# Decoder layer on one core: the second norm's row statistics are computed later, and six instead of four groups of a transpose go over DMA

## The reference

```python
x = x + attn(layernorm(x), w_qkva, gamma)          # stage 1
x = x + xattn(layernorm(x), context, Wq, Wkv, null_kv, Wout, ln_scale, ln_bias)
x = x + ffn(layernorm(x), w_gate, w_up, w_down)

def layernorm(x, eps=1e-5): return (x - mean(x)) / sqrt(var(x) + eps)
def attn(x, w_qkva, gamma):
    xn = x / max(norm(x), 1e-12) * sqrt(256) * gamma
    q, kv, a = split(xn @ w_qkva, 3)
    a = sigmoid(a)                                  # h[t] = a[t] * h[t-1] + kv[t] along the 1024 rows
    return q * scan(a, kv)
def xattn(x, context, ...):                         # 16 heads of 64, 64 context rows and a null key
    ...                                             # softmax(q k^T / 8) v, Wout, a layer norm of the result
def ffn(x, ...):                                    # ternary weights, rows quantised to 8 bits
    ...                                             # down(silu(gate(x)) * up(x))
```

## Time and profile before

| what | value |
|---|---|
| runs | 485.0, 485.03, 488.04 us; median 485.03 |
| profiled execution, its own time | 486.71 us |
| its span, first to last instruction | 484.8 us, so 1.9 us lie around it |
| mean granted TensorE clock | 0.992 |
| busy: PE, DVE, ACT, POOL | 94%, 84%, 71%, 70% of the span |
| chain that ended last | PE 81%, DVE 6%, POOL 5% |

### The profile page before, as it was taken

How to read it: one execution, slowest core, us unless ns; L and a number is a source line. 1 busy time by engine, 2 the same in 40 slices (tenths; PEclk the granted TensorE clock), 3 DMA queues, 4 the chain that set the end, 5 groups by cost and what they waited for, 6 DMA issues and landing times.

```text
span 484.8 us, 8018 instructions
## 1 busy us (share of the span) xinstructions
PE 455.8 (94%) x2520; PEld 358.9 (74%) x2548; DVE 407.0 (84%) x882; ACT 343.0 (71%) x442; POOL 341.5 (70%) x495
## 2 busy tenths in 40 slices
PE   1999999999999999999999999999999999999674
PEld 0777888877877788787877878778787777876332
DVE  4689998997755888998998989989899898997784
ACT  4456756757735456888888888888888888887460
POOL 2234458978880678888878788787887778878850
PEclk9999999999999999999999999999999999999988
DMA  8995014463000000023214222121221312212254
GB/s 262 325 372 212 1 26 63 87 125 94 1 1 1 1 1 11 7 49 45 49 39 51 49 45 49 40 60 39 43 50 39 61 39 45 50 39 62 49 119 89
DMA packets 75577, 33.82 MB, mean 70 GB/s; under 512 B 58128, under 2 KB 73744, under 8 KB 75536
## 3 DMA queue, kind: packets, MB, share of 16 engines
q1 hardware_dynamic: 75536, 33.31, 28.9%
HBM read 15.21 MB, written 4.19 MB: 40 GB/s over the span
## 4 chain that ended last, share of the span: by engine, by line
PE 81%; DVE 6%; POOL 5%; DMA 2%; ACT 2%; issue 2%; another core or an unknown queue 0%; SPq 0%; POOLq 0%; DVEq 0%; ACTq 0%
PE psum L1429 32%; PE psum L1465 12%; PE psum L1713 10%; PE psum L1718 10%; PE psum L1451 3%; PE psum L1690 3%; PE psum L1698 3%; PE psum L1580 2%; PE psum L1561 2%; PE psum L1500 2%; DMA gcol<-in_L_attn_gamma_dram 1%; PE psum L1543 1%; DMA region_d<-region_d 1%; PE psum L1710 1%; PE psum L1484 1%
## 5 line engine op out<-in xcount | busy, mean ns | idle before, releaser
L672 POOL TENSOR_TENSOR region_d<-region_d,rden 128x1024 f32<-128x1024 f32 x30 | 57.1, 1905 | 13.5 <-DVE rden L1230 13.1
L1713 PE MATMUL psum<-VW,region_d 128*128 128x256 f32 x256 | 60.7, 380 | 0.2
L1718 PE MATMUL psum<-VW,region_d 128*128 128x256 f32 x256 | 60.5, 379 | 0.0
L1210 DVE TENSOR_REDUCE mx<-psum 128x8 f32<-128x512 f32 x64 | 44.0, 687 | 13.1 <-PE psum L1429 12.0
L1429 PE MATMUL psum<-Mhi,xT2hi 128*128 128x512 f32 x128 | 53.5, 418 | 0.9 <-DVE xT2lo L1186 0.9
L1718 PEld LDWEIGHTS psum<-VW,region_d 128*128 128x128 f32 x256 | 48.6, 190 | 6.6
L1255 DVE SCALAR_TENSOR_TENSOR region_c<-psum,hzw,region_c 128x1024 f32<-128x1024 f32 x32 | 41.1, 1283 | 13.6 <-ACT region_c L910 13.3
L1713 PEld LDWEIGHTS psum<-VW,region_d 128*128 128x128 f32 x256 | 46.3, 190 | 6.4 <-ACT region_d L985 0.6
L1429 PE MATMUL psum<-Mhi,xT2lo 128*128 128x512 f32 x128 | 50.4, 394 | 0.0
L1429 PE MATMUL psum<-Mlo,xT2hi 128*128 128x512 f32 x128 | 50.1, 391 | 0.0
L602 POOL TENSOR_TENSOR pw_out<-pw_in,expo 128x8 f32<-128x8 f32 x8 | 13.2, 1648 | 44.0 <-DVE pw_in L1085 44.0
(11 more groups left out here) (171 smaller groups left out, 1213.8 us busy)
## 6 DMA issues: line engine op xcount, KB each, us to landing
out_dram<-xs SPq DMA_DIRECT2D x32, 128.0 KB, 2.0
xs<-in_x_dram SPq DMA_DIRECT2D x1, 2560.0 KB, 13.2
VW<-in_L_xattn_Wkv_dram SPq DMA_DIRECT2D x1, 2048.0 KB, 13.4
region_b<-in_L_xattn_Wkv_dram SPq DMA_DIRECT2D x1, 2048.0 KB, 17.2
xs<-in_x_dram SPq DMA_DIRECT2D x3, 512.0 KB, 6.8
region_w<-in_L_ffn_w_gate_dram SPq DMA_DIRECT2D x2, 512.0 KB, 9.7
region_w<-in_L_ffn_w_up_dram SPq DMA_DIRECT2D x2, 512.0 KB, 7.8
region_w<-in_L_ffn_w_down_dram SPq DMA_DIRECT2D x8, 128.0 KB, 5.5
```

The lines of the kernel that those rows point to most:

```text
L672: pool.tensor_tensor(p_of(t).rearrange("p (h j) -> p h j", j=MK), e[:, :, 0:MK], rden[:, v, :].unsqueeze(2).broadcast_to([P, H, MK]), ALU. ...
L1210: dve.tensor_reduce(mx[:, hh, :], scores, AX.X, ALU.max).then_inc(max_done, 1)
L1713: pe.matmul(bank(7, D), pT[:, pair, :], VW[:, batch(n), pair, :], start=False, stop=False)
L1718: mm = pe.matmul(bank(7, D), pT[:, pair, :], VW[:, batch(n), pair, :], start=False, stop=pair == HC - 1)
```

## The change

WHOLE_Y becomes 2: groups 2 and 3, too, are split in planes by ACT, turned by SP's DMAs, and merged and added by POOL. The statistics of the second norm leave steps 2 to 6 of stage 1. Those of group 0 stand in step 7 and those of group 1 in step 8, those of groups 2 to 5 between the `put_keys_lo` of the fold, those of group 6 behind `put_values_first(1)` and those of group 7 behind the transposed rows of tiles 2 and 3 (`xT2_lesser(1, 1)`). POOL's powers for them move along. ACT waits for six groups where it waited for eight, and for all eight in step 8 of the last loop.

```diff
-        WHOLE_Y = 4
+        WHOLE_Y = 2
...
@@ POOL, stage1
-                if exists(g - 2, NG - 1):
-                    deviation2(g - 2)
+                if g == NG or g == NG + 1:
+                    deviation2(g - NG)
...
                     for plane in range(2):
-                        pool.wait_ge(y_plane_T[plane], 16)
+                        if plane == 0:
+                            pool.wait_ge(x1_done, g - 1)
+                        pool.wait_ge(y_plane_T[plane], 16 * (g - WHOLE_Y))
                         pool.tensor_copy(merged_plane(g - 1, plane), turned_plane(plane)).then_inc(y_merged, 1)
-                    pool.wait_ge(y_merged, 2)
+                    pool.wait_ge(y_merged, 2 * (g - WHOLE_Y))
...
@@ POOL, the fold
-            split_kvw(WHOLE)
-            split_kvw(WHOLE + 1)
-            for i in range(WHOLE + 2, HC + 5):
+            for i in range(WHOLE, HC + 5):
                 split_kvw(i)
-                if i == HC + 2:
-                    deviation2(NG - 1)
+                if i in (5, 7, 9, 11):
+                    deviation2((i - 1) // 2)
...
             for pair in range(2, HC):
                 pool.wait_ge(wout_summed, pair - 1)
                 pool.tensor_tensor(wsum, wsum, wout[:, pair, :], ALU.add).then_inc(wout_summed, 1)
+            deviation2(6)
             split_kvw(HC + 5)
...
             split_kvw(2 * HC - 2)
             split_kvw(2 * HC - 1)
             probabilities(1)
+            deviation2(7)
...
@@ ACT
-            act.wait_ge(nmr2_done, NG)
+            act.wait_ge(nmr2_done, 6)
             norm2(4, 0)
...
+                if n == 8:
+                    act.wait_ge(nmr2_done, NG)
...
@@ DVE, stage1
-                if exists(g - 2, NG - 1):
-                    stats2(g - 2)
+                if g == NG - 1:
+                    stats2(0)
+                if g == NG:
+                    shift2(0)
+                    stats2(1)
...
-                if exists(g - 2, NG - 1):
-                    shift2(g - 2)
...
@@ DVE, the fold
                 put_keys_lo(i)
+                if i == 0:
+                    shift2(1)
+                    stats2(2)
+                if i == 1:
+                    shift2(2)
+                if i == 2:
+                    stats2(3)
                 if i == 3:
+                    shift2(3)
                     add_y(NG - 1)
                 if i == 4:
-                    stats2(NG - 1)
-                if i == HC - 1:
-                    shift2(NG - 1)
+                    stats2(4)
+                if i == 5:
+                    shift2(4)
+                if i == 6:
+                    stats2(5)
+                if i == 7:
+                    shift2(5)
...
                 exp_sum_reciprocal(t, t)
                 if t == 0:
                     put_values_first(1)
+                    stats2(6)
+            shift2(6)
             put_values_first(2)
             xT2_lesser(1, 1)
+            stats2(7)
             dve.wait_ge(vnull_hi, 1)
             row = slice(DH // 2, DH // 2 + 1)
...
             put_values_first(3)
+            shift2(7)
```

## The result

The changed kernel takes 496.05 us (median of four executions, 494.97 to 498.52), the kernel before 485.01 us on the same chip: ratio 1.0224 [1.02, 1.0248], so 11.0 us slower. Its profiled execution took 496.08 us with a span of 494.3 us, against 486.71 and 484.8.

A forecast was written before the change was run, and what follows sets the result against it. PE, busy for 94% of the span, was taken as the bound. The terms -1.8 + 1.4 + 3.9 + 0 + 2.3 + 5.0 + 2.0 = +12.8 us against the median 485.0 gave 497.8 us, range 490.5 to 503.

The forecast's parts named there:

- 1, PE's transposes: Stage 1: groups 2 and 3 each lose eight PE transposes, 0.9 us a group, -1.8 us in all.
- 2, the add in step 2: Stage 1, step 2: without the power ahead of it, POOL's add holds up DVE; the step grows by 1.4 us.
- 3, the merges in steps 3 to 5: Stage 1: in each step a POOL merge shuts out DVE's last small instruction for 1.3 us, +3.9 us (0 to 7.8).
- 4 and 5, the fold's start and keys: Fold up to its keys: start taken as 0, added DVE statistics among the keys +2.3 us.
- 6, group 6's statistics: Fold: split_kvw(13) stands behind a power waiting for stats2(6), delaying fold_values(2); largest term, +5.0 us.
- 7, group 7's statistics: End of fold: stats2(7) ahead of put_values_first(3), for which PE's transposes wait without slack; +2.0 us.
- rival that the fold hides the statistics: Fold: DVE takes the statistics in idle time, POOL is never held up; 484.6 or 483.2 us, chance 0.04.
- the first rival: Stage 1: merges miss DVE's five instructions, as planes land late or ACT splits later in step 4; 493.9 us, chance 0.27.
- the second rival: Stage 1: both merges go ahead of L1112, DVE's last small instruction; another 3.9 us, 501.7 us, chance 0.14.
- for longer or not at all: Sign of failure: the prediction is wrong if POOL's merges hold DVE for longer than counted or not at all.
- Part 5: Keys of the fold: three more stats2 and four more shift2, 8.4 us against 5.1 us idle DVE time; +2.3 us.
- part 4: Start of the fold: POOL's first split_kvw behind group 1's statistics and power; -0.9 to +0.5 us, taken as 0.

The follow-up runs named there:

- e3: Changed kernel, with POOL's adds and merges of steps 2 to 5 of stage 1 waiting for DVE's five small instructions: 493.56 us.
- e1: Changed kernel, with POOL's power for group 6 moved behind split_kvw(15), ahead of probabilities(1): 492.55 us.
- e2: Changed kernel, with stats2(6) moved ahead of put_values_first(1) on DVE, POOL's order unchanged: 491.38 us.
- e4: Changed kernel, with group 7's statistics, power and shift2 moved into the first steps of the last loop: 492.61 us.
- e6: Kernel before with WHOLE_Y = 2 alone (planes for groups 2 and 3), all statistics staying in stage 1: 487.2 us, ratio 1.0035.
- e7: Changed kernel with WHOLE_Y = 4, so the statistics move but PE turns groups 2 and 3 as before: 497.56 us.
- e8: Kernel before with WHOLE_Y = 2 and POOL's add and merges of steps 1 to 5 waiting for DVE's five instructions; no statistics move: 485.17 us.
- e9: As e8, with DVE's shift2 moved to the next step, behind the inputs of the first norm's power: 485.67 us, ratio 1.0014.

## Why the prediction was right, and where its terms were not

The forecast was 497.8 us, and 496.05 came. Its terms against the profile after (each the difference of a stretch's length to that of before):

| term | forecast | measured | by |
|---|---|---|---|
| 1, PE's transposes | -1.8 | -1.74 | steps 3 and 4 |
| 2, the add in step 2 | +1.4 | +1.11 | step 2; e3 takes it back |
| 3, the merges in steps 3 to 5 | +3.9 | +2.25 | step 5 alone; e3 takes back 2.08 |
| 4 and 5, the fold's start and keys | +2.3 | +0.1 | last y1 to `fold_values(1)` |
| 6, group 6's statistics | +5.0 | +5.10 | `fold_values(1)` to `(2)`; e1, e2 |
| 7, group 7's statistics | +2.0 | +1.79 | `fold_values(2)` to the transposes; e4 |
| not forecast: start of stage 1, loop, tail | 0 | -0.5, -0.1, +1.5 | |

**Right.** Parts 1, 2, 6 and 7 hold within 0.3 us. Part 1 shows by itself in step 3 of e6, 9.33 us. The mechanisms of the others were shown by undoing each: the power that shielded DVE from the add (e3, e7), the split that waits behind a power behind `stats2(6)` (e1, e2), the statistics ahead of the last copies (e4). The rival that the fold hides the statistics fell where the prediction said it would be decided, at `kv_T(13)`.

**Part 3 was right in kind and mis-sized.** I counted one merge against one instruction in each of three steps. What came is nothing in steps 3 and 4 (the first rival: the margin was 0.1 us, as it says, and fell to the other side by 0.12 us in step 3, and by 0.79 in step 4) and two holds in step 5 (the second rival's loss in one step, though not its form: the first merge held L1115 and the second L1119). That the three steps have one form was the wrong assumption, and by its own sign ("for longer or not at all") the prediction failed in this part. What parts the steps is small: the first merge began 4.53 us after ACT's split of y1 began in step 3, and 4.39 in step 5, with the first of DVE's five instructions 3.6 us behind that split in both. In step 4 ACT split later, as the rival had it: there the five came 2.8 us behind, and the merge 4.41. So tenths of a microsecond decided, and that this part came out between its two ends is luck.

The Trainium skill (SBUF — State Buffer, Who interferes with whom) says that a VectorE instruction with two inputs in SBUF and a GpSimd instruction that reads SBUF exclude each other, and that the one issued first goes first. Step 5 agrees: the merge began at 72.03, and L1115, from 72.09, ended at 73.33, where half of the two merges' 2.59 us is over. POOL's powers don't agree (and below).

L1119 then ended at 74.58, with the second merge. So between two POOL instructions in a row one waiting DVE instruction got its turn, and two merges cost DVE two of its own.

**Part 5 was mis-sized.** DVE's last `put_keys_lo` ended 20.29 us after `kv_T(4)` began, before 19.02: it was late by 1.3 us and not by 3.3. The additions took no less than I priced (four `stats2` of 1.96 to 2.17 us, shifts of 0.55 to 0.96); the room was larger than the 5.1 us that I counted, by a 0.9 us wait for POOL's power among others. PE waited 0.89 us ahead of its scores, for `xT2lo` and not for the keys. And the fold began 0.75 us sooner after the last y1, inside the range of part 4. No run takes these two apart further.

**A step that was too narrow.** Part 1 says that taking the statistics out of stage 1 returns nothing by itself. That holds for four groups turned by PE. With six groups as planes it returns 0.9 us in each of steps 4 and 5, since `shift2` is then held by the add (e6, e8); e9 shows that moving that one instruction does it, too, in those steps.

**Not forecast.** The tail was 1.5 us longer than in the profile before. The three profiles of e9 show that this happens between executions of one kernel; whether the change makes the lower clock likelier isn't shown. The forecast's terms come to 8.6 us and not to 12.8. The median lies nearer to the forecast, 11.0 above that of before, since the tail added 1.5 us, and since the execution profiled before stood 1.7 us above its median while the one after stood at it. The terms by themselves are 4.2 us off; that the forecast is off by only 1.8 is luck to that part.

## What to carry to other kernels

An instruction that waits ahead of another in an in-order queue can be a shield: before moving it, look at what it kept back, and if that holds back an engine on the critical path, put a wait there by design. Statistics whose operands are ready early should stand where the producer is free, but never ahead of work that someone waits for: behind a copy that waits for PE, 2 us of DVE became 5 us of PE by way of one POOL instruction. And read an edit by the stretch that holds it, since the ends of two executions of one kernel differ by more than the edit.

## What the runs showed that I had not expected

- POOL's power doesn't hold DVE's small instructions. In e9, L1114 (two operands in SBUF) takes 0.16 us at 59.18 us inside the power of 58.71 to 59.72; the earlier trace rows show the same. An add, a product or a 16-bit copy on POOL held them for 1.2 to 2.35 us.
- DVE held the power, though. Before the change it takes 1.92 us in place of 1.01 at 104.55, where DVE had begun to clip weights 0.17 us ahead of it, for 1.22 us, and it ends 0.87 us after that; the power at 91.17 us, beside another such row, takes 1.91:

```profile
104.38 1.22 DVE L1031 TENSOR_SCALAR VW<-region_w 128x2048 bf16<-128x2048 f32 x1
```

- PE's waits have a price beyond their length. Behind a stretch in which PE was busy for 2.78 of 6 us, `fold_values(2)` took 3.52 us at half clock in place of 1.96 (e4), and e7 lost 1.2 us at the same place; the kernel after, with waits as long, didn't lose it.
- The tail took 37.8 to 42.2 us over thirteen profiles of eleven kernels with the same instructions in it, a spread wider than what parts 2 and 3 measured together.
